# The distance-attention stage: where a pair's operands are prepared, and how its small products are grouped

## The reference

```python
P = X @ W_in + b_in
Q, K, V, G = jnp.split(P, splits, axis=-1)          # for each of 16 heads
d2 = q2[..., :, None] + k2[..., None, :] - 2.0 * qk
W = jnp.power(EPS + jnp.sqrt(jnp.maximum(d2, 0.0)), -2)
W = W / (EPS + jnp.sum(W, axis=-1, keepdims=True))
A = jnp.einsum('hbts,hbse->hbte', W, V)
H = G * A
return H @ W_out + b_out                            # heads joined
```

## Time and profile before

| | |
|---|---|
| runs | 2405.41, 2406.41, 2406.35 us; median 2406.35 |
| profiled execution | 2405.06 us, span 2403.4 us |
| TensorE matmul, whole span | 2235.0 us busy (93%) |
| ScalarE, whole span | 1630.8 us (68%) |
| VectorE, whole span | 950.3 us (40%) |
| GpSimd, whole span | 476.3 us (20%) |
| distance stage | about the first 468 us |

### The profile page before, as it was taken

How to read it: one execution, slowest core, us unless ns; L and a number is a source line. 1 busy time by engine, 2 the same in 40 slices (tenths; PEclk the granted TensorE clock), 3 DMA queues, 4 the chain that set the end, 5 groups by cost and what they waited for, 6 DMA issues and landing times. The chain is left out here.

```text
span 2403.4 us, 30487 instructions
## 1 busy us (share of the span) xinstructions
PE 2235.0 (93%) x12206; PEld 769.8 (32%) x12206; DVE 950.3 (40%) x1489; ACT 1630.8 (68%) x1295; POOL 476.3 (20%) x254
## 2 busy tenths in 40 slices
PE   8999999899979988999899999999999987999898
PEld 3333333344446632222311111111111122222466
DVE  7766676235441156666211111111111115887111
ACT  4998889633333223555599999999999964666533
POOL 0776665200100024666300000000000000000000
PEclk8999999999989998999999999999999996999999
DMA  1000000036644002000100010010000000000010
GB/s 43 9 5 5 5 1 1 27 140 213 208 159 160 26 0 71 1 1 1 23 24 1 1 43 1 1 43 1 1 1 1 1 2 9 1 1 1 21 35 26
DMA packets 29133, 79.00 MB, mean 33 GB/s; under 512 B 3600, under 2 KB 18976, under 8 KB 26928
## 3 DMA queue, kind: packets, MB, share of 16 engines
q1 hardware_dynamic: 15032, 30.71, 4.1%
q0 software_dynamic: 4384, 29.56, 3.5%
q10 hardware_dynamic: 9592, 16.96, 1.9%
HBM read 71.68 MB, written 5.59 MB: 32 GB/s over the span
## 5 line engine op out<-in xcount | busy, mean ns | idle before, releaser
L1889 ACT ACTIVATE crat_E<-banks 128x1536 f32<-128x1536 f32 x536 | 741.7, 1460 | 22.1 <-PE banks L1780 6.8
L1805 PE MATMUL banks<-crat_E,crat_vst 128*32 128x512 f32 (+1 forms) x3264 | 436.3, 607 | 0.5 <-ACT crat_E L1889 0.4
L1780 PE MATMUL banks<-crat_Q,mid_arena 52*128 52x512 bf16 x1600 | 322.7, 385 | 19.5 <-ACT crat_E L1889 15.3
L1916 DVE COPY crat_vst<-all_crossV 128x96 f32<-128x96 f32 x136 | 34.3, 253 | 635.5 <-PE banks L1805 635.4
L550 POOL TENSOR_TENSOR dist_wsum<-dist_wsum,dist_D 128x1024 f32<-128x1024 f32 x88 | 208.1, 2364 | 7.8
L1509 ACT ACTIVATE rotat_E<-banks 128x1024 f32<-128x1024 f32 x128 | 124.0, 1021 | 116.1 <-PE banks L1393 116.0
L405 DVE TENSOR_SCALAR dist_D<-banks,dist_k 128x512 f32<-128x512 f32 x256 | 178.8, 746 | 54.7 <-PE banks L229 53.6
L1780 PEld LDWEIGHTS banks<-crat_Q,mid_arena 52*128 52x128 bf16 x1600 | 59.3, 93 | 435.3 <-ACT crat_E L1889 300.9
L1575 DVE TENSOR_REDUCE rotat_mx<-banks 128x1 f32<-128x512 f32 x256 | 163.5, 685 | 70.0 <-PE banks L1364 68.8
L1509 ACT ACTIVATE lastat_E<-banks 128x1024 f32<-128x1024 f32 x128 | 123.9, 1020 | 85.6 <-PE banks L1385 85.6
L1575 DVE TENSOR_REDUCE lastat_mx<-banks 128x1 f32<-128x512 f32 x256 | 162.4, 685 | 37.8 <-PE banks L1364 35.1
(11 more groups left out here) (271 smaller groups left out, 2807.1 us busy)
## 6 DMA issues: line engine op xcount, KB each, us to landing
mlp_M<-in_mask POOLq DMA_DIRECT2D x28, 800.5 KB
mid_arena<-cross_k SPq DMA_DIRECT2D x42, 204.0 KB
moe_W<-in_experts SPq DMA_DIRECT2D x16, 512.0 KB, 3.6
mid_arena<-in_rot_tables ACTq DMA_DIRECT2D x8, 1024.0 KB, 19.2
mlp_C<-in_ctx SPq DMA_DIRECT2D x17, 384.0 KB, 4.5
cross_k<-mlp_kp ACTq DMA_DIRECT2D x17, 288.0 KB, 2.3
mlp_row<-in_mask POOLq DMA_DIRECT2D x1, 3202.0 KB, 12.7
mlp_M<-in_mask POOLq DMA_DIRECT2D x1, 3202.0 KB
```

The source lines that it names most:

```text
L1780: last = pe.matmul(PS[:, 3 * (at % 2) + k, :], K[s:s + ROWS, 2 * (g % 2) + pair, c * P:(c + 1) * P], Q[s:s + ROWS, 2 * g + pair, qh * HALF ...
L1805: last = pe.matmul(PS[32 * j:32 * j + 32, 6 + ps % 2, :], vst[keys, (ps * STEPS + c // 3) % 3, c % 3, j, :], E[keys, at // 3 % NE, at % 3, ...
L1889: act.activation(flat(E[:, at % NE, :, :]), flat(PS[:, 3 * (at % 2):3 * (at % 2) + 3, :]), ACT.Exp, scale=CROSS_SCALE).then_inc(s_e, 1)
```

## The change

Q, K, the key norms and the query norms have two buffers, chosen by the pair's parity, and the preparation of pair b+1 moves in between the distances of pair b: q behind chunk 0, the query norms behind chunk 1, k behind chunk 2, the key norms behind chunk 3, values and gates behind chunk 7. The sums of pair b-2 come behind chunk 4. Value product c of pair b-2 stands ahead of the distances of chunk c, all eight. For pairs 0 and 1, whose preparation has no distances around it or follows pair 0's, the order is q, query norms, k, key norms. The squares share one buffer. The query norms are made on all 128 partitions, a copy of each head's three rows for either half h, and the 3-row product of half h takes rows 64h + 32s. The copy p0 and the buffer H are gone: the chain works in the square buffer and in q2, and the gated output is written over `rec`. Ones are taken from `onesd`, which holds 1/128, and the logarithm of the totals gets a scale of 128. The value bias comes by pair (two buffers) instead of at once. On ScalarE the first step of the inverse of pair p-1 stands ahead of the second head's logarithms, and on GpSimd the gates stand inside the first head's sums. The sums of pair 6 follow all eight of its value products.

```diff
+        of = norms(0, "q", "q2", "k", "k2")
+        for c in range(NT):
+            of += dist(0, c)
+        of += norms(0, "v", "g") + norms(1, "q", "q2", "k", "k2", "v", "g")
+        for b in range(1, PAIRS):
+            after = {0: norms(b + 1, "q"), 1: norms(b + 1, "q2"), 2: norms(b + 1, "k"), 3: norms(b + 1, "k2"), SUMMED: sums(b),
+                     NT - 1: norms(b + 1, "v", "g")}
+            for c in range(NT):
+                of += dist(b, c) + after.get(c, [])
+        return of + sums(PAIRS) + sums(PAIRS + 1)
+
+    SUMMED = 4
+    TURN = {e: i for i, e in enumerate(order())}
...
-        bv = n.sb("bv", [P, PAIRS * P])
-        selq = n.sb("selq", [P, D0])
+        bv = n.sb("bv", [P, 2, P])
+        selq = n.sb("selq", [P, P])
...
-        Q = n.sb("Q", [P, T])
-        K = n.sb("K", [P, T])
-        sq = n.sb("sq", [P, 2, T])
+        Q = n.sb("Q", [P, 2, T])
+        K = n.sb("K", [P, 2, T])
+        sq = n.sb("sq", [P, T])
...
+        q2 = n.sb("q2", [P, 2, T], BF16)
...
-                sp.dma_start(bv[:, :], w["bv"]).then_inc(s_bv, 16)
                 sp.dma_start(wp[:, 1, :], w["wpair"][1]).then_inc(s_w[1], 16)
+                for b in range(2):
+                    sp.dma_start(bv[:, b, :], w["bv"][:, b * P:(b + 1) * P]).then_inc(s_bv[b], 16)
...
                     sp.wait_ge(s_made, TURN[b - 2, "g"] + 1)
                     sp.dma_start(wp[:, b % 2, :], w["wpair"][b]).then_inc(s_w[b % 2], 16)
+                    sp.wait_ge(s_taken, TURN[b - 2, "v"] + 1)
+                    sp.dma_start(bv[:, b % 2, :], w["bv"][:, b * P:(b + 1) * P]).then_inc(s_bv[b % 2], 16)
...
-
-                def norms(b):
+                def project(b, k):
+                    if k == "q":
+                        pe.wait_ge(s_w[b % 2], 16 * (b // 2 + 1))
+                    i, at = "qk".index(k), room(b, k)
+                    for h in range(2):
...
                     pe.wait_ge(s_sq, 2 * b + 1)
                     for h in range(2):
...
+                    for h in range(2):
+                        at = room(b, ("d", c, h))
+                        for s in range(2):
+                            pe.matmul(PS[:, at + s, :], K[D0 * s:D0 * s + D0, b % 2, c * P:(c + 1) * P],
+                                      Q[D0 * s:D0 * s + D0, b % 2, h * HALF:(h + 1) * HALF], start=True, stop=False)
+                        if c == 0 and h == 0:
+                            pe.wait_ge(s_q2, b + 1)
+                        for s in range(2):
+                            r = D0 * h + 32 * s
+                            last = pe.matmul(PS[:, at + s, :], onesb[r:r + 3, :], q2[r:r + 3, b % 2, h * HALF:(h + 1) * HALF],
+                                             start=False, stop=True)
+                        last.then_inc(s_made, 1)
...
-                        of = pe.matmul(PS[:, Y + h, :], wout[:, p, :], half(H, h), start=(p == 0), stop=(p == LAST),
+                        of = pe.matmul(PS[:, Y + h, :], wout[:, p, :], half(rec, h), start=(p == 0), stop=(p == LAST),
...
-                for b in range(BODIES - 1):
-                    if b < PAIRS:
-                        project_qk(b)
-                    if b == 0:
-                        pe.wait_ge(s_const, 4 * 16)
-                        pe.wait_ge(s_set, 4)
-                    if b >= 3:
-                        projection(b - 3)
-                    if b >= 2:
-                        values(b - 2, 0)
-                        values(b - 2, 1)
-                    if b < PAIRS:
-                        norms(b)
-                    if b >= 2:
-                        sums(b - 2)
-                    if b >= 2:
-                        values(b - 2, 2)
-                        values(b - 2, 3)
-                    if 0 < b < PAIRS:
-                        project_vg(b)
+                project(0, "q")
+                pe.wait_ge(s_const, 4 * 16)
+                pe.wait_ge(s_set, 3)
+                query_norms(0)
+                project(0, "k")
+                key_norms(0)
+                for c in range(NT):
+                    distances(0, c)
+                project_vg(0)
+                project(1, "q")
+                query_norms(1)
+                project(1, "k")
+                key_norms(1)
+                project_vg(1)
+                for b in range(1, PAIRS):
                     for c in range(NT):
-                        if b >= 2 and c < PIECE:
-                            values(b - 2, PIECE + c)
-                        for h in range(2 if b < PAIRS else 0):
-                            distances(b, c, h)
-                    if b == 0:
-                        project_vg(b)
+                        if b >= 2:
+                            values(b - 2, c)
+                        if b >= 3 and c == 0:
+                            projection(b - 3)
+                        distances(b, c)
+                        if c in (0, 2) and b < LAST:
+                            project(b + 1, "qk"[c // 2])
+                        if c == 1 and b < LAST:
+                            query_norms(b + 1)
+                        if c == 3 and b < LAST:
+                            key_norms(b + 1)
+                        if c == SUMMED and b >= 2:
+                            sums(b - 2)
+                    if b < LAST:
+                        project_vg(b + 1)
+                for c in range(NT):
+                    values(LAST - 1, c)
+                    if c == 0:
+                        projection(LAST - 2)
+                sums(LAST - 1)
...
+                def squared(b, k):
+
+                    i, to = "qk".index(k), (Q, K)["qk".index(k)][:, b % 2, :]
+                    of = made(b, k)
+                    if k == "q":
+                        own.up(dve.tensor_scalar(to, of, bias[:, 0, b:b + 1], None, ALU.add))
+                    else:
+                        own.up(dve.tensor_scalar(to, of, bias[:, 1, b:b + 1], -2.0, ALU.add, ALU.mult))
                     own.done()
+                    dve.scalar_tensor_tensor(sq[:, :], of, bias[:, i, b:b + 1], to, ALU.add, ALU.mult).then_inc(s_sq, 1)
+                    dve.wait_ge(s_sq, 2 * b + 1 + i)
                     dve.sem_inc(s_taken, 1)
+
+                def query_norms(b):
+
+                    to = q2[:, b % 2, :]
+                    of = made(b, "q2")
+                    own.up(dve.tensor_copy(to, of))
                     own.done()
+                    dve.scalar_tensor_tensor(sq[:, :], to, rows[:, 0:1], of, ALU.mult, ALU.add).then_inc(s_taken, 1)
+                    dve.wait_ge(s_taken, TURN[b, "q2"] + 1)
+                    own.up(dve.tensor_copy(to, sq[:, :]))
                     own.done()
+                    dve.scalar_tensor_tensor(to, to, rows[:, 1:2], sq[:, :], ALU.mult, ALU.add).then_inc(s_q2, 1)
+
+                def key_norms(b):
                     of = made(b, "k2")
+                    dve.tensor_copy(flat(k2[:, b % 2, :, :]), of[:, 0:2 * NT]).then_inc(s_taken, 1)
                     dve.wait_ge(s_taken, TURN[b, "k2"] + 1)
...
-                    if p:
-                        dve.wait_ge(s_proj, p)
-                    dve.tensor_tensor(H[:, :], flat(PS[:, 4:6, :]), rec[:, :], ALU.mult).then_inc(s_h, 1)
+                    dve.tensor_tensor(rec[:, :], flat(PS[:, 4:6, :]), rec[:, :], ALU.mult).then_inc(s_h, 1)
...
+                squared(0, "q")
+                query_norms(0)
+                squared(0, "k")
+                key_norms(0)
+                for c in range(NT):
+                    for h in range(2):
+                        distance(0, c, h)
+                values_gates(0)
+                squared(1, "q")
+                query_norms(1)
+                squared(1, "k")
+                key_norms(1)
+                values_gates(1)
+                for b in range(1, PAIRS):
+                    for c in range(NT):
+                        for h in range(2):
+                            distance(b, c, h)
+                        if c in (0, 2) and b < LAST:
+                            squared(b + 1, "qk"[c // 2])
+                        if c == 1 and b < LAST:
+                            query_norms(b + 1)
+                        if c == 3 and b < LAST:
+                            key_norms(b + 1)
+                        if c == SUMMED and b >= 2:
+                            totals(b - 2)
                     if b >= 2:
                         gated(b - 2)
+                    if b < LAST:
+                        values_gates(b + 1)
+                totals(LAST - 1)
+                gated(LAST - 1)
                 finish()
...
                     for s in range(2):
+                        if s and p:
+                            inverse(p - 1, 0)
                         for i in range(2):
                             act.wait_ge(s_root, rooted(p, s, i))
                             act.activation(piece(p, s, i), piece(p, s, i), ACT.Ln, bias=eps[:, 0:1]).then_inc(s_log, 1)
-                        if s and p:
```

(22 more changed lines are left out.)

127 lines of the change are left out of this document (30 added, 97 removed).

## The result

The changed kernel takes **2471.07 us** (median of 4 runs, 2468.7 to 2473.4) where the kernel before takes 2406.16 beside it: a ratio of 1.027, 95% interval 1.0252 to 1.0288. It is slower by 65 us. I had forecast 2442, with a range that ended at 2456. The sign and its cause (a late start, a first body stretched by preparation, ScalarE behind at the end) were right, the size was not: I had forecast a loss of 36 us, and 29 more came on top of it.

What follows compares the result with a forecast made beforehand. TensorE was taken to set the pace mid-stage, busy 53.1 of 54.6 us a body. The profiled 2405.1 plus 33.6 (later last power) plus 3.4 (two clock falls) gave 2442.1, said as 2442, range 2425 to 2456.

Steps and rivals of the forecast that it cites:

- The start: Start of the distance stage: query norms ahead of the key projection put the first distance at 27.2 us, +6.9.
- Body 1: Pair 1's distances, with pair 2's preparation between them, take 38.4 us against 23.6: +14.8.
- chain 4.5: VectorE's chain of operations after the query norms takes 4.5 us.
- T2: Start of the first value product of body 2, forecast at 119.0 us.
- The bodies: Bodies of the distance stage with full preparation and output projection take 54.0 us each, only 0.5 less than before.
- two falls: TensorE's granted clock falls in some bodies, not all: two falls at 1.7 us each, +3.4.
- the wait behind the key norms is gone: Argument against a clock fall in every body: only 0.2 us of idle is left before the key norms.
- rival (a): The clock falls in every body: five more falls at 1.7 us each, total 2450; chance 0.17.
- Where the stall goes: TensorE's stall moves from the norms to the key projection, 1.45 us a body, released by VectorE's evacuation.
- ScalarE: ScalarE idles about 6 us a body ahead of the inverse's logarithm, not ahead of its roots in pair 3 and later.
- T7: Start of body 7's first value product, forecast at 387.2 us; ScalarE's last power then ends at 485.8.
- Nothing for 128 rows, product groups, bias pieces, the dropped buffer: Small parts: these four cost or gain nothing; the groups could save at most 0.8 us a body, taken as 0.

Runs made afterwards that it cites:

- run 4: Changed kernel with pairs 0 to 2 prepared in the order of the kernel before and body 1's distances in a row: 2450.0 us.
- run 6: run 4 with VectorE's query chain split, third operation behind chunk 2 ahead of the key squares, fourth behind chunk 3: 2433.9 us.
- run 12: run 6 with chunk 4's value products put among the key-norm products in two adjacent pairs: 2427.1 us, ratio 1.0084 to the kernel before.
- run 5: Changed kernel with the weight sums moved from behind chunk 4 to behind chunk 0: 2479.9 us.
- run 8: run 6 with two added full-height 256-column products among the key norms of each later pair: 2436.3 us.
- run 1: Changed kernel with GpSimd's sums of the weights cut to 16 of 1024 columns: 2461.8 us.
- run 9: Kernel before with chunk 2's value products put singly among the next pair's key-norm products: 2409.8 us, ratio 1.0006.
- run 11: Kernel before with the value products of chunks 2 and 3 put in adjacent pairs among the key-norm products: 2397.6 us, ratio 0.9962.
- run 3: Changed kernel with the query chain's third and fourth operations moved behind chunks 5 and 6: 2465.0 us.
- run 2: Changed kernel with zero-weight filler products, five ahead of the key projection and two among the key norms: 2471.8 us.
- run 7: Changed kernel with both query halves back in one product group, on rows 32s: 2475.0 us.

## Why the prediction was wrong in size

The last power tells the parts: 515.7 minus 24.9 (start and body 1, run 4) minus 14.8 (chain, run 6) minus 4.9 (falls at the key norms, run 12) minus 19.0 (what run 12 still has) is 452.1, before's. The 19.0 is 11.3 us by which pair 6's last distance comes later, since a pair's distances are spread over a body, and 7.7 us more from there to the last power; run 5, where early sums brought that stretch from 100.3 to 93.4, says that these 7.7 are the late sums. No run has both run 12's bodies and early sums, so this split is worked out and not measured, and some 2 us of the 11.3 are the wait in body 3 that the restored start brings. The parts are differences of single profiled executions, and good to 2 or 3 us: the start of run 8 lay 2.4 us off that of run 6 with the same instructions in it.

- **The start**: right to 1 or 2 us. First distance at 29.1 us (forecast 27.2, before 20.29); TensorE's first distance of pair 1 at 79.1 (78.2).
- **Body 1**: mis-sized. Distances took 45.2 us, not 38.4. The term was "chain 4.5"; it was 7.8, since GpSimd was adding at that time. The step that failed is the one that took chain durations from the earlier trace rows, where GpSimd does not meet the chain. Run 1, with the chain back at 4.5, still takes 42.1. Most of these other 3.5 us are half clock behind the wait and at the key norms: the projection takes 3.78 instead of 1.88, the norms 3.27 instead of 1.95. T2 was 128.07 instead of 119.0, 9 us of the miss: 0.9 from the start, 6.8 from the distances, and 1.3 between the last distance and T2.
- **The bodies**: mis-sized, 58.5 us instead of 54.0. The failed step is the clock: "two falls" in the stage, since "the wait behind the key norms is gone". Run 6 has no wait around the key norms and still falls; runs 9, 11 and 12, which put 512-column products between them, do not in their later bodies. So the norms bring it without a wait. They do not do so every time: one body of run 3 had unmixed norms and no fall, and what decides this stays open. The wait that I had placed ahead of the key projection brings more half clock: in the changed kernel it stood behind the wait of 2.1 us in all four bodies that have one, and was gone when the wait was filled (run 2) or removed (run 6). Where half clock lies and how long it lasts varies from body to body, also in runs 1 and 3; its sum in the changed kernel does not, and costs 1.6 + 1.5 us a body. GpSimd makes that wait 0.7 longer (2.13 against 1.37 in run 1). The 1.45 that I gave for it did not follow from my own terms, 4.5 + 1.41 - 4.72, which make 1.2. The remaining 0.7 us of the 4.5 I did not take apart. Over five bodies this is 21.5 us. My rival (a) had one fall a body, and so ended at 2450.
- **Where the stall goes**: right, at the key projection, released by VectorE's evacuation (L430), in every body.
- **ScalarE**: right in kind. It waits once a body, ahead of the inverse, not ahead of its roots; 11.1 us instead of 6, since bodies are 4.5 longer. From T7 to the last power I had 98.6 us, measured 515.7 - 417.75 = 98.0.
- **Nothing for 128 rows, product groups, bias pieces, the dropped buffer**: right. The first two are seen (the chain's first operation takes 1.22 us on 128 rows, as on 64 in the earlier trace rows; run 7), the last two only in that no row waits for them; no run undoes them alone.

In the sum: 9.1 + 21.5 - 0.6 = 30.0, less the 3.4 us that I had added for two falls, gives 26.6 of the 27 us by which the profiled execution passed the forecast. None of the signs that I had named for being wrong came: body 1 took over 30 us, ScalarE was held by the totals' copy, and no body fell under 52. They looked only for a loss smaller than forecast.

## What to carry to other kernels

Where the last engine in a chain (ScalarE here) has work for two stages left, what counts is when its input is complete, not when the next stage begins: spreading producer steps over a body costs the end, even when the bodies become shorter (run 12). When a step is moved under other work, take its duration from rows in which the same neighbours run: two operations that only read SBUF grew by 3.3 us beside GpSimd. Before a stretch of tiny products is priced by its own row, read the row behind it for the clock, and mix wide products that have to run anyway between them, neighbours that share the array kept together.

## What I had not expected of the hardware

- The granted clock falls behind sixteen two-column records though TensorE had not waited over 0.3 us (row 297.06 of run 6: 3.63 us instead of 1.94; not in every body, see run 3). The Trainium skill's TensorE: Matmul & The Clock Gate, "Why this matters for your kernels", advises against idle gaps between bursts; here a gap was not needed.
- Value products of two heads, each on 64 columns, cost 1.9 us for eight records in a row, and 0.96 us for two records that stand alone (run 9).
- One cast took 0.69, 1.45, 1.97 or 2.50 us, depending on whether and when GpSimd was adding (runs 1, 5 and the changed kernel).
